# Five preparation stages of a twelve-layer decoder kernel, done inside the layers before them

## What is computed

```
x = layernorm(x + part(x, ...))        # 12 times; x is 128 sequences x 64 rows x 128 features, float32
L0 attn, L0 xattn, L0 ffn(8 experts), L1 attn(GQA), L1 xattn(mask), L1 ffn(8 experts),
L2 attn, L2 xattn, L2 ffn(8 blocks), L3 attn(recurrent), L3 xattn(cell), L3 ffn
```

## Time and profile before

| what | us |
|---|---|
| median of 3 runs | 5046.01 (5044.64 to 5055.25) |
| the profiled execution's own time | 5045.63 |
| its span in the trace | 5043.9 |
| PE busy in the span | 4368.0 (87%) |
| DVE busy in the span | 3502.5 (69%) |
| ACT, POOL busy in the span | 2334.7 (46%), 1235.0 (24%) |
| before L0x: span without PE, from L0a's last row to L0x's first instruction | 364.7 to 405.2 |
| before L1x: the same | 2034.7 to 2065.5 |
| before L3x: the same | 4443.1 to 4525.4 |

### The profile page before, as it was taken

One profiled execution on the slowest core, in us unless ns is written; L12 is line 12 of the kernel. 1 busy time (PEld: TensorE's weight loads), 2 busy tenths in 40 slices (PEclk: granted clock), 3 DMA queues, 4 the chain that ended last, 5 costly groups with the idle time before them and its releaser, 6 DMA issues. The chain is left out here.

```text
span 5043.9 us, 147959 instructions
## 1 busy us (share of the span) xinstructions
PE 4368.0 (87%) x54045; PEld 3195.0 (63%) x54086; DVE 3502.5 (69%) x8221; ACT 2334.7 (46%) x4101; POOL 1235.0 (24%) x2155
## 2 busy tenths in 40 slices
PE   6986988999899998698997999899899968829986
PEld 5764666556577887476776666577676434416765
DVE  5887883555477777587883555588787667758985
ACT  3554552222244443365783333355686445505553
POOL 1222331000000000122451000133222234405653
PEclk9997997999999999799997999999999989959998
DMA  2011110000000000111000000000011100020001
GB/s 76 13 30 47 37 33 23 1 0 0 11 2 0 0 0 1 43 42 33 18 17 18 1 0 0 4 14 13 24 32 35 50 7 0 0 53 26 23 18 34
DMA packets 138993, 97.90 MB, mean 19 GB/s; under 512 B 38425, under 2 KB 133153, under 8 KB 138273
## 3 DMA queue, kind: packets, MB, share of 16 engines
q1 hardware_dynamic: 138784, 95.06, 6.4%
HBM read 61.43 MB, written 4.19 MB: 13 GB/s over the span
## 5 line engine op out<-in xcount | busy, mean ns | idle before, releaser
L1338 ACT ACTIVATE L1m_G<-L1m_psY,L1m_B 128x512 f32<-128x512 f32 x256 | 175.9, 687 | 286.5 <-PE L1m_psY L1292 277.7
L1003 DVE TENSOR_TENSOR L0f_SG<-L0f_SG,L0f_psY 128x512 f32<-128x512 f32 x176 | 120.8, 686 | 247.7 <-PE L0f_psY L947 247.4
L1268 PEld LDWEIGHTS L1m_psO<-L1m_W,L1m_G 128*128 128x128 f32 x2048 | 243.8, 192 | 64.5 <-issue 35.9
L986 ACT ACTIVATE L0f_SG<-L0f_psY 128x512 f32<-128x512 f32 x176 | 105.1, 597 | 356.8 <-PE L0f_psY L945 356.8
L1268 PE MATMUL L1m_psO<-L1m_W,L1m_G 128*128 128x128 f32 x2048 | 248.2, 276 | 13.1 <-DVE L1m_ACC L1389 13.1
L1292 PE MATMUL L1m_psY<-L1m_XT,L1m_W 128*128 128x512 f32 x512 | 246.0, 604 | 0.8 <-ACT L1m_XT L1320 0.7
L958 PEld LDWEIGHTS L0f_psO<-L0f_W,L0f_G 128*128 128x128 f32 x1408 | 182.0, 191 | 102.0 <-issue 61.9
L1389 DVE SCALAR_TENSOR_TENSOR L1m_ACC<-L1m_psO,L1m_gate,L1m_ACC 128x128 f32<-128x128 f32 x448 | 126.0, 343 | 163.5 <-PE L1m_psO L1268 161.4
L958 PE MATMUL L0f_psO<-L0f_W,L0f_G 128*128 128x128 f32 x1408 | 188.4, 277 | 17.1 <-DVE L0f_G L1007 10.9
L947 PE MATMUL L0f_psY<-L0f_XT,L0f_W 128*128 128x512 f32 x352 | 180.6, 595 | 2.3 <-issue 0.2
L945 PE MATMUL L0f_psY<-L0f_XT,L0f_W 128*128 128x512 f32 x352 | 181.5, 598 | 0.7 <-ACT L0f_G3T L974 0.7
(11 more groups left out here) (646 smaller groups left out, 12892.1 us busy)
## 6 DMA issues: line engine op xcount, KB each, us to landing
L0a_KB<-L0a_KT SPq DMA_DIRECT2D x128, 32.0 KB, 1.8
stats_rms_chunk<-in_ctx SPq DMA_DIRECT2D x8, 512.0 KB, 4.0
L0x_CS<-in_ctx SPq DMA_DIRECT2D x32, 128.0 KB, 2.2
L0x_CR<-in_ctxT SPq DMA_DIRECT2D x32, 128.0 KB, 2.3
L0x_KB<-L0x_KT SPq DMA_DIRECT2D x128, 32.0 KB, 1.8
L1x_MI<-in_mask SPq DMA_DIRECT2D x32, 128.0 KB, 3.3
L1x_CR<-in_ctxT SPq DMA_DIRECT2D x32, 128.0 KB, 3.0
L1x_KB<-L1x_KT SPq DMA_DIRECT2D x128, 32.0 KB, 1.8
```

Of the source, the lines that this page charges most:

```text
L986: nc.scalar.activation(SG[:, yb, :], psY[:, yb, 0, :], ACT.Silu).then_inc(S["silu"].sem, 1)
L1003: nc.vector.tensor_tensor(SG[:, yb, :], SG[:, yb, :], psY[:, yb, 1, :], ALU.mult).then_inc(S["product"].sem, 1)
L1268: i_ = nc.tensor.matmul(psO[:, ob, j, :], G[:, m % 2, c, j * P:(j + 1) * P], W2[:, m, c, :], start=c == 0, stop=c == fc - 1)
L1338: i_ = nc.scalar.activation(G[:, m % 2, c, :], psY[0:fw, yb, 0, :], ACT.Relu, bias=B1[:, m, c:c + 1])
```

## The change

What the five stages did is put elsewhere.

- `attention("L0a")` gets `tally=True`. SP loads the context rows of each pair into `CS`. POOL squares 128x256 numbers, adds neighbours in three steps (widths 128, 64, 32), and scales: once per pair for the context (even slots, at the end) and once for the rows that DVE has just finished (odd slots, at the end). DVE takes the reciprocal of each (128x32) at the end of its slots. The pipeline drains two slots later. `head_roots()` replaces `source_stats("rms")` and holds two square roots on ACT, 128x1024 each.
- `packed_experts` gets a block part for SP, which loads the mask (two transfers) and the context rows of a batch (one), and `side_work` on DVE in chunk 6 of each batch: the mask addends, and the row statistics of the context.
- `expert_blocks`: SP also loads the cells of each batch (two transfers), and DVE makes the cell mask of the batch before at the end of its slot.
- `recurrent_block`: its first block also does the whole of `fold_norms` and the scale, root and inverse of the context's variances. POOL copies each batch's row variances (128x4) after `row_root`.
- `row_roots()` replaces `source_stats("ln")` for X: after a normalisation to variance v/(v+eps) the mean is zero and the inverse deviation follows from v. DVE does five operations on 128x64 and ACT one root. L3x then only multiplies X by it (one POOL operation per pair instead of two).

The calls:

```diff
-        attention("L0a", Wm("L0q"), ..., mask=static)
-        source_stats("rms")
+        attention("L0a", Wm("L0q"), ..., mask=static, tally=True)
+        head_roots()
...
-        key_masks("mask")
...
         recurrent_block()
-        key_masks("cell")
-        source_stats("ln")
-        fold_norms()
+        row_roots()
```

In `attention`:

```diff
-            drain = 5 + e + late + (1 if affine is not None else 0)
+            drain = 5 + e + late + (1 if affine is not None else 0) + (2 if tally else 0)
...
-                        if turn_c and R_.ok:
+                        if (turn_c or tally) and R_.ok:
-                            made(sp, "ctx_normed", R_.p - 1)
+                            made(sp, "tallied_c" if tally else "ctx_normed", R_.p - 1)
                             pace(sp, S)
                             sp.dma_start(CS[:, R_.u, :, :], io["ctx"][bass.ds(R_.p * 256, 256), :]...
...
+                    def mean_squares(p, src_, n, dst, read, done):
+                        tally_ = ("tally_c", "tally_x")[n]
+                        pace(g, S)
+                        nc.gpsimd.tensor_tensor(SQ[:, n, :].rearrange("p (t d) -> p t d", t=2), src_, src_, ALU.mult).then_inc(S[tally_].sem, 1)
+                        for k, (a, b) in enumerate(((SQ, Q4), (Q4, Q2), (Q2, Q1))):
+                            made(g, tally_, 4 * p + k + 1)
+                            pair = a[:, n, :].rearrange("p (g h w) -> p g h w", g=2 * HEADS, h=2)
+                            nc.gpsimd.tensor_tensor(b[:, n, :].rearrange("p (g w) -> p g w", g=2 * HEADS), pair[:, :, 0, :], pair[:, :, 1, :], ALU.add).then_inc(S[tally_].sem, 1)
+                        made(g, tally_, 4 * p + 4)
+                        made(g, read, p - 1)
+                        pace(g, S)
+                        nc.gpsimd.tensor_scalar(dst, Q1[:, n, :], 1.0 / HD, RMS_EPS, ALU.mult, ALU.add).then_inc(S[done].sem, 1)
...
+                        Z, Y = T + 4, T - 7
+                        if tally and T.par == 0 and Z.ok:
+                            parity_wait(g, "rows_in", Z, 16)
+                            mean_squares(Z.p, CS[:, Z.u], 0, MC[:, Z.u, :], "rooted_c", "tallied_c")
+                        if tally and T.par == 1 and Y.ok:
+                            made(g, "out_rows", Y.p + 1)
+                            mean_squares(Y.p, X[:, bass.ds(Y.p * 2, 2), :], 1, MS[:, Y.u, :], "rooted_x", "tallied_x")
...
+                        for V_, par, mean, st, tallied, rooted in ((T + 3, 1, MC, stat2, "tallied_c", "rooted_c"), (T - 8, 0, MS, stat, "tallied_x", "rooted_x")):
+                            if tally and T.par == par and V_.ok:
+                                made(dv, tallied, V_.p + 1)
+                                pace(dv, S)
+                                nc.vector.reciprocal(st[:, bass.ds(V_.p * 2, 2), :].rearrange("p t h -> p (t h)"), mean[:, V_.u, :]).then_inc(S[rooted].sem, 1)
```

`head_roots`, and the side work of L0f:

```diff
+        def head_roots():
+            with nc.Block() as block:
                 @block.scalar
                 def _(act):
+                    for st in (stat2, stat):
+                        nc.scalar.activation(st[:, :, :], st[:, :, :], ACT.Sqrt)
...
+                    def side_work(B):
+                        half_b = B.c // 2 if B.i is None else B.i + B.c // 2
+                        dv.wait_ge(side_in(B).sem, side_in(B).base + 48 * (half_b + 1))
+                        nc.vector.tensor_scalar(maskk[:, B.tiles(), :], MK[:, B.u, :, :], 0.0, NEG, ALU.is_equal, ALU.mult)
+                        for j in range(TB):
+                            m = nc.vector.bn_stats(cst[:, j, :], CH[:, B.u, j, :])
+                        m.then_inc(S["side_bn"].sem, 1)
+                        dv.wait_ge(S["side_bn"].sem, S["side_bn"].base + B.b + 1)
+                        pace(nc.vector, S)
+                        for j in range(TB):
+                            m = nc.vector.bn_aggr(cag[:, j, :], cst[:, j, :])
+                        m.then_inc(S["side_aggr"].sem, 1)
+                        dv.wait_ge(S["side_aggr"].sem, S["side_aggr"].base + B.b + 1)
+                        nc.vector.tensor_copy(stat2[:, B.tiles(), 0:2], cag[:, :, :]).then_inc(S["side_used"].sem, 1)
...
+                                if c == 6:
+                                    side_work(B)
```

In L2f (SP and DVE, at the ends of their slots), and in L3a:

```diff
+                            made(sp, "mask_made", B.b - 1)
+                            pace(sp, S)
+                            for s in range(2):
+                                rows = io["cell"].rearrange("(t s k) -> s t k", s=2, k=SEQ)[s, B.rows, :]
+                                sp.dma_start(MK[64 * s:64 * s + 64, B.u, :, :], rows.partition_broadcast(64)).then_inc(mask_in(B).sem, 16)
...
+                        if A.ok:
+                            dv.wait_ge(mask_in(A).sem, mask_in(A).base + 32 * (A.e + 1))
+                            made(dv, "mask_made", A.b)
+                            nc.vector.tensor_tensor(KEEP[:, :, :], MK[:, A.u, :, :], cellq[:, A.rows].unsqueeze(2).to_broadcast([P, TB, SEQ]), ALU.not_equal).then_inc(S["mask_keep"].sem, 1)
+                            made(dv, "mask_keep", A.b + 1)
+                            nc.vector.scalar_tensor_tensor(maskk[:, A.rows, :], KEEP[:, :, :], NEG, causal[:, :].unsqueeze(1).to_broadcast([P, TB, SEQ]), ALU.mult, ALU.add).then_inc(S["mask_made"].sem, 1)
...
+                    var = stat2[:, :, 1:2]
+                    nc.vector.tensor_scalar(var, var, 1.0, LN_EPS, ALU.mult, ALU.add).then_inc(S["stat2_var"].sem, 1)
+                    for n, (w, g_, _, _) in enumerate(folded):
+                        nc.vector.tensor_scalar(wp[:, n, :], Wm(w), C(g_), None, ALU.mult)
+                    for n, b in enumerate(("L3av", "L3ao", "L3bv")):
+                        m = nc.vector.tensor_scalar(colb[:, n, :] if n < 2 else bvb[:, :], ident, 0.0, C(b), ALU.mult, ALU.add)
+                    m.then_inc(S["fold"].sem, 1)
+                    dv.wait_ge(S["stat2_root"].sem, S["stat2_root"].base + 1)
+                    nc.vector.reciprocal(var, var)
+                    dv.wait_ge(S["fold_pe"].sem, S["fold_pe"].base + 1)
...
+                            nc.gpsimd.tensor_copy(stat[:, E.rows, 1], ag[:, E.u, :, 1])
```

`row_roots`:

```diff
+            var, part = stat[:, :, 1], stat[:, :, 2]
...
+                    nc.vector.tensor_scalar(part, var, 1.0, LN_EPS, ALU.mult, ALU.add).then_inc(S["x_var"].sem, 1)
+                    done(1)
+                    nc.vector.reciprocal(part, part).then_inc(S["x_var"].sem, 1)
+                    done(2)
+                    nc.vector.tensor_tensor(part, part, var, ALU.mult).then_inc(S["x_var"].sem, 1)
+                    done(3)
+                    nc.vector.tensor_scalar(part, part, 1.0, LN_EPS, ALU.mult, ALU.add).then_inc(S["stat_var"].sem, 1)
+                    dv.wait_ge(S["stat_root"].sem, S["stat_root"].base + 1)
+                    nc.vector.reciprocal(var, part)
```

More of the change, by code:

```diff
@@ L202, in attention @@
         def attention(L, q, k, v, o, qs=None, ks=None, gq=None, gqs=None, gk=None, gks=None, bq=None, bqs=None, bk=None, bks=None, bv=None, bo=None,
-                      cq=0, ck=0, cross=False, norm=None, mask=None, keymask=False, ln_o=False, affine=None, keep=None):
+                      cq=0, ck=0, cross=False, norm=None, mask=None, keymask=False, ln_o=False, affine=None, keep=None, tally=False):
             mem = Memory(nc, L)
@@ L233, in attention @@
             OL = mem.sb("OL", [P, 2, D])
+            SQ, Q4, Q2, Q1, MS = (mem.sb(n, [P, 2, HEADS * 2 * w]) for n, w in (("SQ", 8), ("Q4", 4), ("Q2", 2), ("Q1", 1), ("MS", 1))) if tally else [None] * 5
+            MC = mem.sb("MC", [P, 2, HEADS * 2]) if tally else None
             psS = mem.pb("psS", [P, 4, 2 * HQ, SEQ])
@@ L816, in _ @@
+        def head_roots():
+            with nc.Block() as block:
                 @block.scalar
                 def _(act):
-                    if norm == "rms":
-                        for k in range(2 * n):
-                            r = k // 2
-                            if k % 2:
-                                act.wait_ge((S["chunk_in1"] if r % 2 else S["chunk_in"]).sem, (S["chunk_in1"] if r % 2 else S["chunk_in"]).base + 16 * (r // 2 + 1))
-                            if after(k - 1):
-                                act.wait_ge(S["chunk_used"].sem, S["chunk_used"].base + k - 1)
-                            src_ = chunk[:, r % 2, :, :] if k % 2 else X[:, r * w:(r + 1) * w, :]
-                            nc.scalar.activation(sq[:, k % 2, :, :], src_, ACT.Square).then_inc(S["squared"].sem, 1)
@@ L896, in batches, with packed_experts, side_in, _ @@
                 slot(Bat(None, c))
-        def packed_experts(L, NCH, W1, W2, XS, XT, SG, G, ACC, st, ag, rt, psX, psY, psG, psO, gate3, G3S, G3T, SEL):
+        def packed_experts(L, NCH, W1, W2, XS, XT, SG, G, ACC, st, ag, rt, psX, psY, psG, psO, gate3, G3S, G3T, SEL, MK, CH, cst, cag):
+            def side_in(B):
+                return S["side_in1"] if B.u else S["side_in0"]
```

(15 more changed lines are left out.)

173 lines of the change are left out of this document (46 added, 127 removed).

## The result

The changed kernel takes 4926.22 us (median of four executions, 4925.33 to 4927.91) against 5046.29 for the one before (four, 5044.64 to 5055.25): 0.9759 of the time, 95% interval 0.9742 to 0.9776. The forecast was 4926.0. That the two agree to 0.2 us is luck: executions of one and the same kernel lie 3 to 11 us apart.

The account below looks back on a forecast made before the run. Inside its layers the kernel runs at or close to PE's pace, with 151.5 us of PE-idle stretches between stages. Savings of 141.6 against +22 (L0a 14, fold 6, L3a 2) net -119.6 from 5045.6: 4926.0 us, range 4915 to 4943.

Parts of the forecast that it names:

- The three stretches: Times without PE work before L0x, L1x and L3x shrink to short remainders, saving 33.2, 30.2 and 78.2 us.
- The fold: L3a's first block takes over the weight folding behind the decay column: +6.0 us, bounds 4 to 8.
- L0f: DVE's side work of 2.1 us per batch fits into 3.0 us lying free: cost 0.
- L2f: Two added DVE operations per batch, 13 us in all, fit into 45 us free: cost 0, at worst 16.
- L3a's batches: POOL's copy of row variances, 0.27 us in each of 16 batches: +2 us, between 0 and 4.3.
- L0a, the reciprocals: The rows' reciprocal stands in L0a's pace-setting loop, 32 x 0.25 = 8 us; the context's costs 0.
- L0a, the lock: DVE row writes held by POOL's small additions in L0a, 0.2 us per pair: 6 us, ends 0 and 29.
- L0a's +14: Whole cost of the additions in L0a, reciprocals 8 plus lock 6 us; between 0 and 50.
- (1): L0a takes the additions free because DVE's waiting absorbs the reciprocal, and L3a's copy is free: 4910 us; chance 0.15.
- (2): In L0a both reciprocals count and additions hold every row write: +50 instead of +14, 4962 us; chance 0.12.
- (3): L0f's side work isn't hidden, queued with the multiplications: 34 us, 4960 us; chance 0.06.
- (4): Slower than before, POOL bounding L0a if a tally takes over 5.6 us; 5126 us at three times the price; chance 0.02.

Follow-up runs that it names:

- experiment 10: Changed kernel with four steps moved (rows' reciprocal to odd slots, roots into L0a's end, last row root earlier, fold ahead of decay column): 4917.8 and 4919.2 us.
- experiment 9: Changed kernel with L0f's row statistics and aggregations done three times per batch (12 and 12 instead of 4 and 4): 4941.1 us.
- experiments 2 to 4: Changed kernel with DVE's L0a reciprocals left out: all 4922.4 us, the rows' 4916.7, the context's 4920.8.
- experiment 6: Changed kernel with the square and three sums of each POOL tally in L0a done twice: 4973.8 us.
- the second profiles: Repeat runs of unchanged kernels: the kernel before, 5049.9 us, and the changed kernel beside the version with four steps moved, 4923.6 us.

## Why the prediction was right, step by step

The mechanisms of the large terms were right, and the size of the sum is right in part by chance: L0a came out 2.7 us cheaper than forecast, L3a's batches 2.0 dearer and the untouched stages 2.2 longer, and these misses nearly cancel (-119.6 forecast, -118.2 measured). The range 4915 to 4943 is a little narrower than its own terms give, 4913 to 4944.

- **The three stretches** (-33.2, -30.2, -78.2): measured -33.1, -30.2, -78.2. They were sums of durations read for the same operations, and nothing else ran in them.
- **The fold** (+6.0): +5.8. Right also in how: a chain behind the decay column. What I hadn't asked is whether it had to stand there; experiment 10 took 2.2 us off by turning the order round.
- **L0f** (0, "3.0 us lie free against 2.1"): 0, with 2.8 free against 1.9. The sum of the two idle pieces, DVE's wait and the time until PE used the product, was the right sum; experiment 9 found the edge where it puts it. **L2f** (0): 157.7 in both.
- **L3a's batches** (+2, by 0.27 us of the copy on the batches' chain): the term failed as a mechanism. The measured 3.6 to 4.0 is near my upper end only by chance: copies as such cost nothing (331.0 with them), and the length has two values that go with the clock, with the copies and without.
- **L0a, the reciprocals** (+8, the rows' in the pace loop, the context's free): which of the two costs is shown by experiments 2 to 4; experiment 10 adds that the rows' reciprocal isn't free in the odd slot either once the context's stands there. The size was off: about 5, not 8 (305.9 to 307.7 without the rows' reciprocals, 311.3 to 312.6 with them; from the second shift to the last, 301.5 and 301.6 in the two profiles of the kernel before, 306.8 and 306.9 in the two of the changed one). I took 0.25 for each of 32 pairs. A pair lost 0.19, and only 29 pairs have their row writes ahead of the last shift, 58 of the 64 writes: 29 x 0.19 = 5.5. Where the other 0.06 of a pair went, no run shows.
- **L0a, the lock** (+6, "each write can be held by at most one of them; I take 0.2 per pair"): 0. The step that failed is the price, not the collision: writes and POOL's additions do meet (157.44 and 157.69), but the writes aren't held: the writes of 0.4 to 0.7 us that the forecast named as a sign didn't come, the longest is 0.361. I had scaled the case of L3f, where POOL's operation is 128x512, down to 128x32. Where a 128x256 square meets the writes, they wait for all of it (experiment 6, and the last write of experiment 10).
- **L0a, left out of the sum**: the start of the stage (+1.4; +0.9 between the second profiles) and the drain (+1.8 as the change's part; +2.0 between the second profiles). I had costed the drain from the last row on and not what happens to the row root before it, though both stand on POOL. So L0a's +14 met a measured +11.3 in the first profiles, made of 5.3 + 1.4 + 1.8 and 2.8 of the clock; the agreement is partly luck. Between the second pair of profiles it is +9.5 (last row write ends at 364.0 and 373.5): 0.9 + 6.6 + 2.0, where 1.2 of the 6.6 are the step from the first shift to the second.
- **The rivals.** (1) L0a free, 4910: refuted for L0a, 5 us for the rows' reciprocals, and right on the copy in L3a; its own reason, that DVE's wait absorbs the reciprocal, is true of the context's. (2) The lock in full, 4962: refuted. (3) L0f's side work exposed, 4960: refuted, with 0.9 us to spare per batch. (4) POOL as the bound, from 5.6 us per tally: the tally measured 2.3. Done twice it takes 4.3 (205.88 to 210.17 in experiment 6), which by its "7.1 us free per pair" should cost 1.5 us per pair; a pair in the middle of the stage took 1.43 more, and POOL's waits for DVE's rotary parts, 2.6 us per pair in the changed kernel, are down to 0.8 us over 13 pairs. The bound is there, where I had put it. (The stretched row writes and a granted clock of 0.96 in place of 1.00 over the stage stand beside it; with POOL hardly waiting for anything, neither is needed for the 1.43.)

The Trainium skill, SBUF — State Buffer, section "SBUF: two separate sides", says that of a VectorE operation in a two-port mode and a GpSimd operation the one that starts first keeps the shared port pair for its whole instruction. By that rule, experiment 6 agrees in size (held 0.65 us beside a square of 0.62), and by it a write that meets an addition of 0.26 or 0.29 could be held for up to that long. None was in the changed kernel (0.361 at most), and in the slot shown it was the addition that took 0.09 longer; so for short instructions this case doesn't bear the rule out. In the two rows of experiment 6 the write's recorded start is 0.02 us earlier than the square's, and yet it was the write that waited; no run here shows when the pair is taken.

## What to carry to other kernels

A stage that leaves most engines idle is worth its whole length, and its price elsewhere is found by asking in which queue, behind which instruction, each moved operation will stand: one reciprocal of 0.35 us per pair of tiles cost about 1 us over 64 tiles in one slot and 5 us in the other, and the first slot had no room for a second. Cost the drain of a pipeline separately from its steady part, with everything that was newly put on the engine that ends it. And take a second profile before giving a meaning to 3 us: here a tail and a stage had two lengths each, with the clock, in the same code or nearly the same, and the step between L0a's first two shifts took 4.3 or 5.8 us with nothing changed.

## What the runs showed of the hardware

- DVE's write from SBUF to SBUF (tensor_scalar, 128x128) waits out a POOL tensor_tensor of 0.62 us beside it, 1.25 us instead of 0.60 for two (experiment 6). Row statistics and a reciprocal beside the same kind of square keep their length, in the tails of the changed kernel and of experiment 10:

```profile
372.72 0.61 POOL L353 TENSOR_TENSOR L0a_SQ<-X 128x256 f32<-128x256 f32 x1 [1.02 <-DVE X L716]
372.99 0.29 DVE L678 BATCH_NORM_STATS2 L0a_st<-L0a_RB 128x6 f32<-128x128 f32 x1
```
```profile
373.03 0.61 POOL L353 TENSOR_TENSOR L0a_SQ<-X 128x256 f32<-128x256 f32 x1
373.21 0.35 DVE L734 RECIPROCAL stat<-L0a_MS 128x32 f32<-128x32 f32 x1 [1.19 <-POOL L0a_MS L361]
```

- The drain of L0a was granted the full clock, 2.4 GHz, until about 9 us after the last shift in one execution of the changed kernel, and until about 3 us after it in another, with the same code; then 1.2 GHz (0.50 in the windows behind). The windows in which it falls, in the first profile (last shift 359.0) and in the second (358.7):

```profile
361.00:363.00 2.00, 1.34 (x7) 1.37 (x8) 0.48 (x3) 0.76 (x3) 0.89 (x2) 0.69 0.03 8
```
```profile
366.70:368.70 2.00, 1.20 (x5) 0.75 (x5) 1.19 (x6) 0.28 (x1) 1.54 (x6) 0.82 0.00 0
```

- Narrow operations on POOL took 0.61 us for the square of 128x256, 0.46 for the sum of 128x128, 0.29 and 0.26 for 128x64 and 128x32, and 0.22 for the scaling of 128x32. I had drawn a line through two widths of other operations and was off by 0.12 at most.
